# A ring of three places instead of four for the injected products of a selective scan

## The reference

```python
proj = xn @ W_in.T                      # x | gate, 2048 channels each
x = silu(conv4(x)); ts, B, C = rms(x @ W_x.T)
dt = softplus(ts @ W_dt.T + b_dt)
for t in tokens:                        # the recurrence, 2048 channels x 16 states
    state = state * exp(dt[t] * A) + (dt[t] * u[t]) * B[t]
    y[t] = sum(state * C[t], over the 16 states)
s = ((y + x * D) * silu(gate)) @ W_out.T
h = silu(qlinear(xn, gate_q)) * qlinear(xn, up_q)
out = x_in + s * silu(qlinear(h, down_q))
```

## Time and profile before

| | before |
|---|---|
| median of 3 runs | 2817.31 us (2815.68 to 2823.78) |
| profiled execution | 2815.07 us |
| its span | 2813.3 us |
| PE busy | 2692.6 us (96%) |
| DVE busy | 2400.2 us (85%) |
| POOL busy | 1990.7 us (71%) |
| ACT busy | 1585.7 us (56%) |
| PE in the chain that ended last | 48% |
| DVE in it | 19% |

### The profile page before, as it was taken

The page is one execution under the profiler, slowest core; times in us unless marked ns, Lnnn a source line. Parts: engine busy times, 40 slices in busy tenths (PEclk is TensorE's granted clock), DMA queues, the critical chain, the costliest instruction groups (busy, mean ns, idle before and its releaser), DMA issues.

```text
span 2813.3 us, 42520 instructions
## 1 busy us (share of the span) xinstructions
PE 2692.6 (96%) x15444; PEld 1562.1 (56%) x15444; DVE 2400.2 (85%) x2913; ACT 1585.7 (56%) x2643; POOL 1990.7 (71%) x946
## 2 busy tenths in 40 slices
PE   6999999599999999999999999989999999999999
PEld 3555555255555555555555555556666665556544
DVE  6887876699999998888888888897999999999910
ACT  4454644566666666767777767654545555445400
POOL 2311232288999988888888978796978888899711
PEclk9999999799999999999999999989999999999999
DMA  7745473455465544444445344664454546756441
GB/s 248 236 162 177 157 283 144 134 186 167 145 189 166 166 142 143 137 152 127 153 137 161 127 148 137 199 169 132 122 155 126 147 120 182 252 158 190 144 118 56
DMA packets 338800, 449.78 MB, mean 160 GB/s; under 512 B 170624, under 2 KB 181120, under 8 KB 334176
## 3 DMA queue, kind: packets, MB, share of 16 engines
q1 hardware_dynamic: 338592, 447.07, 52.0%
HBM read 313.08 MB, written 133.91 MB: 159 GB/s over the span
## 4 chain that ended last, share of the span: by engine, by line
PE 48%; DVE 19%; issue 7%; DMA 3%; ACT 1%; POOL 1%; SPq 1%; DVEq 0%; POOLq 0%; ACTq 0%
PE bank L1673 10%; DVE inj L1407 10%; PE turned L1603 10%; PE bank L1645 9%; PE bank L1647 9%; DVE ysum L1425 6%; PE bank L1721 6%; PE back L1687 2%; DMA h_s<-work 2%; DVE work L1461 1%; PE bank L1656 1%; DMA work<-in_wout 1%; PE back L1614 1%; POOL inj L1545 1%; DVE us L1434 0%
## 5 line engine op out<-in xcount | busy, mean ns | idle before, releaser
L1545 POOL TENSOR_TENSOR inj<-dub,bb 128x2048 f32<-128x2048 f32 x256 | 1161.9, 4539 | 309.3 <-PE turned L1603 240.1
L1407 DVE TENSOR_TENSOR_SCAN inj<-decay,carry,inj 128x512 f32<-128x512 f32 x1024 | 1283.0, 1268 | 32.6 <-POOL inj L1545 18.1
L1260 ACT ACTIVATE decay<-dtb,aneg 128x512 f32<-128x512 f32 x1024 | 704.7, 688 | 701.3 <-DVE inj L1407 695.2
L1603 PE MATMUL turned<-ident,inj 128*128 128x128 f32 x4096 | 626.8, 276 | 37.5 <-DVE inj L1407 24.2
L1603 PEld LDWEIGHTS turned<-ident,inj 128*128 128x128 f32 x4096 | 503.1, 142 | 251.2 <-DVE inj L1407 77.9
L1425 DVE SCALAR_TENSOR_TENSOR ysum<-turned,cT,ysum 128x512 f32<-128x512 f32 x721 | 527.1, 731 | 115.2 <-PE turned L1603 114.0
L1645 PE MATMUL bank<-xx,work 128*128 128x512 f16 x1408 | 533.6, 379 | 1.0 <-ACT work L1273 1.0
L1647 PE MATMUL bank<-xx,work 128*128 128x512 f16 x1408 | 533.6, 379 | 0.0
L1626 PE MATMUL bank<-xx,work 128*128 128x512 f16 x1536 | 374.3, 380 | 27.7 <-POOL work L1523 27.7
L743 PE MATMUL main<-xx,ww 128*128 128x512 f16 x1536 | 343.9, 381 | 2.8 <-DVE xx L502 1.5
L1560 POOL TENSOR_TENSOR ysum<-ysum,work 128x512 f32<-128x512 f32 x239 | 306.2, 1281 | 10.5 <-ACT work L1298 10.5
(11 more groups left out here) (144 smaller groups left out, 2864.7 us busy)
## 6 DMA issues: line engine op xcount, KB each, us to landing
bb<-bt_s SPq DMA_DIRECT2D x128, 512.0 KB, 5.8
ww<-w_s SPq DMA_DIRECT2D x48, 512.0 KB, 4.0
work<-in_gu_q SPq DMA_DIRECT2D x88, 256.0 KB, 3.4
h_s<-work SPq DMA_DIRECT2D x88, 256.0 KB, 3.8
u_s<-ub SPq DMA_DIRECT2D x64, 256.0 KB, 4.4
dt_s<-mx SPq DMA_DIRECT2D x16, 1024.0 KB, 4.6
dtb<-dt_s SPq DMA_DIRECT2D x32, 512.0 KB, 8.8
gs_s<-work SPq DMA_DIRECT2D x64, 256.0 KB, 5.9
```

Source lines behind the costliest of these rows:

```text
L1260: act.activation(decay[j % 2][:, :], dtb[:, step % 2, j, :], ACT.Exp, scale=aneg[:, step % G * J + j, n:n + 1]).then_inc(s_dec, 1)
L1407: v.tensor_tensor_scan(inj[:, s % RING, j, :], decay[j % 2][:, :], inj[:, s % RING, j, :], carry[:, step % G * J + j, n:n + 1], ALU.mult, ...
L1545: pool.tensor_tensor(inj[:, e % RING, :, :], dub[:, step % 2, :, :], bb[:, e % 8:e % 8 + 1, :].broadcast_to([P, J, T]), ALU.mult).then_inc ...
L1603: mm = pe.transpose(turned[t % 2][:, j * P:(j + 1) * P], inj[:, s % RING, j, t * P:(t + 1) * P], ident[:, :])
```

## The change

The constant RING is 3 where it was 4. The ring `inj` has three places of 128x2048, the two waits at L1537 and L1538 go by three, and so does every index into the ring (L1384, L1407, L1545, L1604). Order and number of instructions stay.

```diff
-RING = 4
+RING = 3
```

## The result

The kernel with three places takes 4270.01 us (median of 4 runs), the kernel before 2818.2 (4 runs): ratio 1.5149, 95% interval 1.5128 to 1.517. The profiled execution took 4268.53 us with a span of 4266.8. One of the four took 5059 us, with a mean granted clock of 0.605 where the others had 0.858, and is not in the ratio.

A forecast was written before the change was run, and what follows sets the result against it. The prediction took the 256 recurrence slots, with POOL's products held by the ring and work queued behind that wait, as the bound. 2815.07 us plus 1112 for longer slots plus 340 for the clock gave 4267, stated as 4270; range 3700 to 4600.

The forecast's parts named there:

- First link: All stages: ACT's `weigh` waits for POOL's addition, queued behind its product; second transpose group at T0+7.3, period 10.8 us.
- T0: Start of a slot's fourth transpose group (`turn(s-1, 3)`), from which the forecast counts its times.
- Second link: Up/gate stage: DVE's write of `hb` waits for POOL's low half of h; next first group at T0+9.6, period 14.6 us.
- The clock: Holes in PE's work drop the granted clock to half speed for 3.5 us, 1.75 us in most slots: +340 us.
- The slots without the clock: Longer slots from both links, the gate store and small terms: gate +262, up/gate +512, down and out +338, together +1112 us.
- SP's link: SP's `load_bb` is answered later, so the gate store behind it lands late for DVE; odd gate slots take 13.0 us.
- the h store: I take nothing: Up/gate stage: h store arrives about when ACT wants its buffer, nothing to half a microsecond; counted as zero.
- The rival with the first link alone: `hb` finds its low half in time; up/gate stage +160 instead of +512, total 3575 to 3800 us; chance 0.1.
- Absorbed wait: Rival: POOL's idle time takes up the lost place, not slower, 2815 us; chance 0.04.
- Clock held: Rival: both links but no fall of the clock, 3927 us, between 3800 and 4100; chance 0.22.
- Clock low most of the time: Rival: both links with transpose path doubled, about 4800 us, taken as over 4600; chance 0.1.
- the contention of GpSimd with VectorE: POOL's products might be shorter beside an idle DVE; at most 10 us over 256 products.

The follow-up runs named there:

- r3_dense_bb: Three places with bb loads one pair later, plus PE running the first gate product piece and the second half of the up/gate unit twice: 4097.5 us.
- r3_add3: Three places, with only POOL's addition made for slot e-3 instead of e-4: 3887.84 us.
- r3_bb: Three places, with only SP's bb loads one pair later: 4289.31 us.
- r4_lag5: Kernel before (four places), with POOL's addition and low half of h made for slot e-5 instead of e-4: 4263.43 us, ratio 1.5125.
- r3_lag3: Three places, with POOL's addition and low half of h made for slot e-3 instead of e-4: 3721.62 us.
- r3_lag3_bb: Three places, with POOL's addition and low half of h at e-3 and SP's bb loads one pair later: 3145.22 us.
- r3_low3_bb: Three places, with only the low half of h at e-3, the addition left at e-4, and bb loads one pair later: 3970.32 us.
- r4_lag3: Kernel before (four places), with POOL's addition and low half of h made for slot e-3 instead of e-4: 3077.88 us, ratio 1.0923.

## Why the prediction was right, and where it was not

The time was forecast at 4270 us and measured at 4270; by stages the sum holds too. Its terms with the clock's share were gate 736 + 56 (56 slots at 1.75, less 42), up/gate 1346 + 154, down 741 + 76, out 392 + 55. Measured: 779, 1516, 819, 443. The mechanism is the forecast one, but that the two numbers agree to the microsecond is luck, as the parts show.

- **First link: right.** Second group forecast at T0+7.3, measured at T0+7.25, odd gate slots forecast at 13.0, measured 12.99. r3_dense_bb gives the gate stage with the clock nearly held and without the store: 690 us, 670 by the sum (14 x 10.8 + 2 x 7.4 over 16, plus 0.1, times 64).
- **Second link: right.** Forecast 9.6 us to the next first group, 10.82 measured with 1.26 for `dub`; 14.66 us a slot with the clock held. r3_add3 shows that the up/gate stage keeps its loss without the first link.
- **The clock: right in kind, too small in size.** It was put at half speed for 3.5 us, that is 1.75 a slot and 340 in all. In the up/gate stage, by the clock's record laid over PE's matmuls, PE worked 381 us at half clock, 4.3 a slot, and so lost about 2.2 (7.11 against 5.0 in the slot above). Of the two cases behind the 3.5, taken as 3.3 and 4.0 us, the clock's record has 3.4 and 4.3; both are from the kernel before, where such holes are rare. In all four stages PE worked 871 us at half clock. Half of that, 435 us, is an estimate of what the clock took, if all of this work was on the path; by stages it is 73, 191, 101 and 70 against 56, 154, 76 and 55 forecast.
- **The slots without the clock: too long by about as much.** What this estimate leaves of the lengths is 706, 1330, 713 and 373 us, against 736, 1346, 741 and 392 forecast. The two errors, about 95 us each, cancel; that is the luck. 9 us of it are a slip in the sum: 14.6 + 0.1 + 0.3 + 0.2 is 15.2, not 15.3. Where the others lie was not traced. (The 5.0 us from first to fourth group does not stand in the earlier trace rows; PE's timeline of that stage has 4.99 as the median.)
- **SP's link: half right.** The store's lateness and the 13.0 us were forecast. But the term was summed as if removing it would shorten the gate stage, by 62 us less 42 of overlap with the clock. r3_bb, which removes it, is 15 us longer there, and r4_lag5 18: the clock takes its place, with 0.80 and 0.79 where the kernel with three places had 0.90. In its odd slots the hole is in two parts (3.62 and 2.06 us above) and the clock stood at 1.00 through both; that this is why it held is argued, not shown. And "the h store: I take nothing" holds only under the first two links. Once they are gone, SP's link is worth 394 us in the up/gate stage (1371 in r3_lag3, 977 in r3_lag3_bb).
- **The fourth link was not seen at all** (ACT's copy of y behind POOL's L1579). It changed nothing in the forecast, since slower links covered it: 11.9 us in 8 times in the kernel with three places, 317.2 in 60 once they were gone.
- **The rival with the first link alone was mis-sized**: 11.3 us a slot in the up/gate stage against 13.7 in r3_low3_bb. It left out PE's wait for ACT's scaling (L1332), the fourth link in front of it, and the clock, which fell to 0.93 there.
- **The rivals' fate.** Absorbed wait: out, and r4_lag3 shows how narrow the slack is. Clock held: out; it would be 3927. Clock low most of the time, forecast near 4800: out at the median, where the mean was 0.858.

The Trainium skill ("TensorE: Matmul & The Clock Gate", "A second HAM failure mode: psum-queue depth-cycling") remarks that the clock swings between its levels under micro-idles while the median matmul looks unchanged. The traces agree, with the clock falling and rising again from slot to slot: the median matmul is 379 ns in both kernels, and the stages run at 0.80 to 0.90.

On the contention of GpSimd with VectorE (the Trainium skill, "GPSIMD Engine Reference", "8. Key points") the kernel with three places gives the other end: with DVE at 57% the products take 4515 ns in the mean, before 4539. That is 6 us in all, within the 10 allowed. It does not test the page's case of two SBUF inputs, since the scans read `decay` from PSUM (L840).

## What to carry to other kernels

Where an engine works through a fixed order, the number of places in a ring is also the distance between its wait and everything queued behind that wait. Before a ring is cut (or a distance changed), list for each instruction behind the wait who needs it and by when; move them all by the same distance, the transfers of the queue that waits for the same counter too, and the place may be free: here 8 KB of each partition for nothing. If only some are moved, the next link sets the slot, so a partial undo tells little about its own worth. The distance can be too short as well: with four places, one iteration less cost 258 us.

## What the runs showed of the hardware that was not expected

More work on PE made the kernel shorter: 1792 extra matmuls in its holes took 192 us off (4289 to 4098), since the granted clock rose from 0.80 to 0.98 in the gate stage. The length of a hole alone does not tell what the clock does. A hole of 3.62 us was passed at full clock in the gate slot shown above, while in r3_bb four holes of 3.6 us stand in a stretch of 55 us at 0.75 (905 to 960 us). In the up/gate stage of the kernel with three places nearly all holes are of 5.3 or 6.5 us; behind 83 of the 88 PE came back to half clock, and it lasted 2.7 to 6 us of work in nearly all of them.
